# Six-piece attribute load and adjacency store, issued between the gathers of a graph network kernel

## The chip, the core and the metric

One NeuronCore of a Trainium2 chip runs the whole program. The metric is the time of one execution on the device, in microseconds (us). Engines: PE (TensorE: matmuls and transposes), DVE (VectorE), ACT (ScalarE), POOL (GpSimd), SP (SyncE, which only issues transfers here). They run side by side and meet through semaphores. Transfers that SP issues go to a queue served by the core's 16 DMA engines (the hardware queue, q1 in the profile); the indirect gathers that POOL issues go to another queue of the same 16 engines (q0).

## What is computed

A layer of graph attention, and then a layer that sums neighbours and edge attributes, over N = 6250 nodes and E = 200,000 edges sorted by target node, 128 channels:

```python
h = relu(layernorm(x))
xp = (h @ W).reshape(n, 4, 32)
e = leaky_relu(a_s[src] + a_d[dst]); alpha = softmax of e over the edges of each dst
x = x + relu(segment_sum(alpha * xp[src], dst) + bias)           # with a self loop per node
h = relu(layernorm(x))
edge_agg = segment_sum(edge_attr @ We + be, dst)
x_comb = concat([h, edge_agg]);  neigh = segment_sum(x_comb[src], dst)
x = x + relu((x_comb + neigh) @ W1 + b1) @ W2 + b2
```

## The kernel before, in words

After a preparation (node table, logits, masks) the kernel works through the sorted edges in NG = 87 groups of GE = 2304 edges, J = 18 edges for each of the 128 partitions. The targets of a group lie in a window of 128 consecutive nodes. Two sets of buffers alternate, b = n mod 2. The first stage (this is where the change lies) does for group n:

- POOL, `gather` (L768): 18 indirect gathers of 128 table rows of 576 B each into V[b] (L776). The burst for group m may refill a third of V[b] when PE has finished the same third of group m-2 (semaphore vm_b, once each six gathers). So beside group n runs the burst of group n+1.
- DVE, `item`: opens the group with the copy into thru4 (L1554), builds the selection matrix (L1400), the marks for the adjacency, the running maximum of the logits (L1569, then L1578 after PE's transpose L1085, then L1583 after PE's L1087), the new peak of each node (L1614 to L1621, after PE's L1098), looks up the shifts and scales the gathered rows (L1667).
- PE, `item`: adjacency products c = 0 to 5 (L1066), transposes L1085 and L1087, the first half of the attribute sums (L1056, selection times attribute rows), the peak merge (L1098, 18 small matmuls), adjacency 6 to 11, the second half of the attribute sums (its last increments am_b), the lookups (L1110), the weighted sums (L1122, in thirds, each increments vm_b), adjacency 12 to 17.
- ACT: copies the adjacency products from PSUM into adjw[b] (semaphore ab_ev, 18 a group; the last six of group n run at the start of group n+1), and the exponentials.
- SP, `item` (L526): every transfer of the stage, in the order of the program. One wait holds everything behind it.

SP's order for group n before the change: peak and dlogit of the window (L472, L473), the rel rows (L477), store the sums of n-1 (L495, when they are merged), store the new peak of n (L482, when DVE has it: mnew_b), the indices of group n+2 (L440, when the gathers of n have landed), the attributes of group n+2 (L443, 1152 KB, 9216 B for each partition, when am_b of n says that the buffer is free), load the sums (L488) and x (L491), store the residual and the projection of earlier groups (L501, L506), store the adjacency of group n-1 (L510, 1543.5 KB, 12348 B for each partition).

A second stage reads the 87 adjacency blocks back and multiplies them with the second layer's rows. It starts when all stores have landed (adj_out). The blocks named "extra" aren't executed with these inputs.

Of the kernel before, what the change touches and what calls it, by code (L numbers as in the profile page):

```python
# [25 lines left out]
J = 18  # L26
# [29 lines left out]
QUART = J // QN  # L56
FIN = 18
MAGIC = 0x5f3759df
ST = TAB + C
# [12 lines left out]
FARHI = 1 << 20  # L72
assert COLS <= 128 and OFF <= 256 and NB * 128 <= NPAD and GE == J * 128
YCH = ((0, 13), (13, 25), (25, 37), (37, 49))
# [3 lines left out]
def gnn_kernel(nc, x, src, dst, attr, W, att_src, att_dst, bias0, We, be, W1, b1, W2, b2, out):  # L78
    ctx = ExitStack()
    with ctx:  # L80
# [213 lines left out]
        def s(name):  # L294
            if name not in S:
                S[name] = sem(name)
            return S[name]
# [4 lines left out]
            fj_in fj_f jsel_b colr_b dl dl_done tab0_out peak_out tab_out sp_turn idx0 idx1 gat0 gat1  # L302
            attr0 attr1 g_started st_load m_store s_load s_store xw_load sel_b drx_b selc_b thru4_b thruT_b
            thru_c cont_b log_b pre1_b tailT_b tails_b cback_b carry_b pre2_b pkl_b pk_b mg_b mgs_b mnew_b nu_b
# [65 lines left out]
        def _(sp):  # L370
# [65 lines left out]

            def load_edges(n, b, it, start):
                after_dma(sp, s(f"gat{b}"), it * J)
                sp.sem_inc(s("sp_turn"), 1)
                sp.dma_start(idx[b][:, :], src[bass.DynSlice(start, GE)].rearrange("(p j) -> p j", j=J))\  # L440
                    .then_inc(s(f"idx{b}"), 16)
                after(sp, s("am_b"), n, 2)
                sp.dma_start(AT[b], attr[bass.DynSlice(start, GE), :].rearrange("(p j) c -> p j c", j=J))\  # L443
                    .then_inc(s(f"attr{b}"), 16)

            sp.sem_inc(s("y_out"), 16)
            for b in range(2):
                load_edges(b, b, 0, b * GE)

# [57 lines left out]

            def store_adjacency(n, b):
                sp.wait_ge(s("ab_ev"), n * J + J)
                sp.dma_start(adj[bass.DynSlice(n, 1), :, :].rearrange("a p c -> (a p) c"), adjw[b].bitcast(BF16))\  # L510
                    .then_inc(s("adj_out"), 16)
# [14 lines left out]
            def item(n, b, it):  # L526
                base = base_of(n)
                load_peak(n, b, base)
                load_rows(n)
                before_first = isinstance(n, int) and n == 0  # L530
                if not before_first:
                    base_before = base_of(n - 1)
                    store_sums(n - 1, base_before)
                store_peak(n, b, base)
                if not isinstance(n, int) or n + 2 < NG - 1:
                    load_edges(n + 2, b, it + 1, (n + 2) * GE)
                elif n + 2 == NG - 1:
                    load_edges(n + 2, b, it + 1, LAST)
                if before_first:
                    sp.wait_ge(s("tab_out"), 32 * (TAB_CHUNKS + 1))  # L540
                load_sums(n, base)
                if not before_first:
                    store_residual(n - 1, base_before)
                if not (isinstance(n, int) and n < 2):
                    store_projected(n - 2, base_of(n - 2))
                if not before_first:
                    store_adjacency(n - 1, 1 - b)

# [11 lines left out]
            store_residual(NG - 1, base)  # L560
            store_adjacency(NG - 1, 0)
            store_projected(NG - 1, base)
# [14 lines left out]

            sp.wait_ge(s("adj_out"), 16 * NG)
            load_adjacency(0, 0)
# [44 lines left out]
            def extra_item(n, b, it):  # L624
                load_edges(n, b, it, extra(sp, 2, n, LAST))
                base = extra(sp, 1, n, N)
                load_peak(n, b, base)
                store_peak(n, b, base)
                load_sums(n, base, True)
                store_sums(n, base)  # L630
                sp.wait_ge(s("s_store"), n * 16 + 16)
                sp.sem_inc(s("sp_turn"), 1)
# [41 lines left out]
        def _(pool):  # L674
# [93 lines left out]
            def gather(b, it, rows, table, index, gat, ix, n=None):  # L768
                pool.wait_ge(s(f"{ix}{b}"), it * 16 + 16)
                pool.sem_inc(s("g_started"), 1)  # L770
                for j in range(J):
                    if n is not None and j % QUART == 0 and not (isinstance(n, int) and n < 2):

                        pool.wait_ge(s("vm_b"), n * QN + (j // QUART + 1 - 2 * QN))
                        pool.sem_inc(s("g_started"), 1)
                    pool.indirect_dma_start(  # L776
# [15 lines left out]
            with pool.If(uncovered(pool) > 0):  # L792
                extra_pairs(pool, item)
                pool.wait_ge(s("tab1_out"), 64)
                pool.sem_inc(s("g_started"), 1)
                for b in range(2):
# [5 lines left out]
                extra_pairs(pool, first_item2)  # L802
                pool.sem_inc(s("g_started"), 1)


        @block.scalar
        def _(act):
# [59 lines left out]
            def item(n, b, it, is_extra=False):  # L867
# [10 lines left out]
                if not is_extra:  # L878
                    after_dma(act, s("adj_out"), n - 1)
                    keep_adjacency(n, b, 0, 12)  # L880
# [64 lines left out]
        def _(pe):  # L945
# [106 lines left out]
            def item(n, b, it, is_extra=False):  # L1052
# [37 lines left out]
                after(pe, s("selc_b"), n)  # L1090
                pe.wait_ge(s(f"attr{b}"), it * 16 + 16)
                after(pe, s("merged"), n, 2)
# [715 lines left out]
```

## Time and profile before

| | us |
|---|---|
| timed runs, median of 3 | 4222.09 (4209.79 to 4226.62) |
| the profiled execution | 4203.44, of it span 4200.3 |
| the first stage's groups | first opened at 120.8, last at 3391.1 |
| mean granted TensorE clock | 0.745 of full speed |

| engine | busy us | share of the span |
|---|---|---|
| PE | 2634.0 | 63% |
| PE weight loads | 2099.8 | 50% |
| DVE | 1797.7 | 43% |
| POOL | 1652.3 | 39% |
| ACT | 1001.7 | 24% |
| DMA, SP's queue / POOL's queue | | 36.1% / 13.2% of 16 engines |

How to read it: no engine is busy most of the time, so shares say little; what counts is who waits for whom inside a group. A timeline row has start, duration, engine, line, operation, output<-input and how many were merged, and in square brackets the idle time before it and what ended it ("issue": nothing that the profile shows; "remote": a semaphore whose sender it can't name). Times in the text such as +11.1 are counted from the opening copy L1554 of the group in question.

### The profile page before, as it was taken

What the parts mean: (1) busy time and instruction counts of PE and PEld (TensorE: products, weight loads), DVE (VectorE), ACT (ScalarE), POOL (GpSimd) and SP (SyncE); (2) the same over time, 40 slices, a digit from 0 to 9 for tenths busy, and PEclk for the clock granted to TensorE, in tenths of its full rate; (3) what the DMA queues carried; (4) which work ended last, traced back from release to release, by engine and by line L of the source; (5) the groups of instructions that cost most, each with busy time, mean ns of one, the idle gap of its engine ahead of it and who ended that gap; (6) DMA issues with size and microseconds to landing.
All of it is one profiled execution on the core that took longest, in us unless ns stands there. A gap on an engine that the chain in (4) does not pass through costs nothing.

```text
span 4200.3 us, 62157 instructions
## 1 busy us (share of the span) xinstructions
PE 2634.0 (63%) x16749; PEld 2099.8 (50%) x16749; DVE 1797.7 (43%) x6117; ACT 1001.7 (24%) x2335; POOL 1652.3 (39%) x1625
## 2 busy tenths in 40 slices
PE   3455555555555555565555555555555559999999
PEld 2343444444444444444344444444444448888887
DVE  6444454445454444444445444444444541111111
ACT  2223223222222222222222222232222230000000
POOL 4544544454444444544455444544454410000000
PEclk7667676667666676666777776667666779999999
DMA  9444444444443444444444444444444446666665
GB/s 183 113 133 123 141 145 143 126 127 143 145 138 116 141 136 130 133 142 137 124 137 145 144 136 124 140 140 136 123 141 144 135 157 221 215 213 221 215 213 180
DMA packets 309819, 630.10 MB, mean 150 GB/s; under 512 B 115675, under 2 KB 239191, under 8 KB 276133
## 3 DMA queue, kind: packets, MB, share of 16 engines
q1 hardware_dynamic: 259679, 514.22, 36.1%
q0 software_dynamic: 50112, 115.56, 13.2%
q8 instruction: 11, 0.18, 0.0%
q14 instruction: 17, 0.14, 0.0%
HBM read 446.35 MB, written 183.24 MB: 150 GB/s over the span
## 4 chain that ended last, share of the span: by engine, by line
PE 42%; another core or an unknown queue 23%; issue 16%; DVE 9%; ACT 5%; SPq 3%; DMA 1%; DVEq 0%; ACTq 0%
PE pv L1184 11%; PE pv L1122 10%; PE pv L1056 8%; PE pt L1184 5%; ACT xsb L809 5%; PE pt L1066 3%; DVE big L1667 2%; PE pa L1066 1%; DVE lks L1650 1%; DVE tabb L1400 1%; PE pa L1110 1%; PE pm L1098 1%; DVE lin L1654 1%; DVE lin L1659 0%
## 5 line engine op out<-in xcount | busy, mean ns | idle before, releaser
L776 POOL DMA_INDIRECT big<-table,idx x1566 | 1615.6, 1032 | 1698.4 <-PE pv L1122 1220.0
L809 ACT ACTIVATE xsb<-pt 128x343 bf16<-128x343 f32 x1044 | 531.5, 543 | 1987.3 <-PE pt L1066 1029.0
L1066 PE MATMUL pt<-tabb 128*128 128x343 bf16 x1044 | 395.4, 381 | 819.9 <-ACT xsb L809 461.6
L1066 PEld LDWEIGHTS pt<-tabb 128*128 128x128 bf16 x1044 | 105.4, 101 | 1053.4 <-ACT xsb L809 577.5
L1056 PE MATMUL pv<-big 128*128 128x128 f32 x3132 | 629.4, 386 | 0.0
L1056 PEld LDWEIGHTS pv<-big 128*128 128x128 f32 x3132 | 613.0, 299 | 1.5
L1122 PE MATMUL pv<-big 128*128 128x133 f32 x3132 | 498.6, 326 | 162.3 <-DVE big L1667 162.3
L1122 PEld LDWEIGHTS pv<-big 128*128 128x128 f32 x3132 | 470.9, 234 | 182.9 <-DVE big L1667 175.5
L1184 PE MATMUL pv<-big,xsb 128*126 128x384 bf16 x2842 | 493.8, 327 | 19.0 <-DVE big L1695 19.0
L1184 PEld LDWEIGHTS pv<-big,xsb 128*126 128x126 bf16 x2842 | 382.8, 136 | 88.2 <-issue 19.0
L1400 DVE TENSOR_TENSOR tabb<-iotah,keyp 128x2064 bf16<-128x2064 bf16 x261 | 320.3, 1227 | 1.4 <-issue 1.1
L1578 DVE TENSOR_TENSOR_SCAN tails<-thruT,pm 4x128 f32<-4x128 f32 x87 | 35.6, 409 | 618.5 <-issue 293.8
L1614 DVE TENSOR_SCALAR pen<-pm 128x1 f32<-128x1 f32 x87 | 13.7, 158 | 665.0 <-remote 549.6
L809 ACT ACTIVATE xsb<-pa 128x343 bf16<-128x343 f32 x522 | 280.2, 537 | 24.6 <-PE pt L1066 12.5
L1184 PE MATMUL pt<-big,tabb 128*126 128x384 bf16 x1421 | 248.4, 326 | 0.0
L1667 DVE TENSOR_TENSOR big<-big,pm 128x768 f32<-128x768 f32 x261 | 233.4, 950 | 26.1 <-ACT pm L809 26.1
L1066 PE MATMUL pa<-tabb 128*128 128x343 bf16 x522 | 199.1, 381 | 40.1 <-issue 28.6
L1710 DVE TENSOR_TENSOR fy<-pa,fxw 128x128 f32<-128x128 f32 x87 | 25.4, 292 | 454.2 <-PE pa L1167 454.2
L1098 PE MATMUL pm<-peaks,selb 128*128 128x13 bf16 x1566 | 72.8, 171 | 226.2 <-issue 191.7
L1184 PEld LDWEIGHTS pt<-big,tabb 128*126 128x126 bf16 x1421 | 190.8, 136 | 33.8
L809 ACT ACTIVATE fhT<-pt,b1s 128x128 f32<-128x128 f32 x87 | 31.9, 367 | 707.1 <-PE pt L1161 707.1
L809 ACT ACTIVATE big<-selb 128x2304 f32<-128x2304 bf16 x87 | 183.2, 2106 | 0.6 <-issue 0.6
(271 smaller groups left out, 2584.0 us busy)
## 6 DMA issues: line engine op xcount, KB each, us to landing
adj<-xsb SPq DMA_DIRECT2D x87, 1543.5 KB
big<-in_edge_attr_dram SPq DMA_DIRECT2D x87, 1152.0 KB, 5.2
xsb<-adj SPq DMA_DIRECT2D x58, 1543.5 KB, 6.7
selb<-rel SPq DMA_DIRECT2D x87, 576.0 KB
tabb<-adj SPq DMA_DIRECT2D x29, 1543.5 KB, 6.7
big<-table,idx POOLq DMA_INDIRECT x1566
state<-sums SPq DMA_DIRECT2D x87, 130.5 KB
sums<-state SPq DMA_DIRECT2D x87, 130.5 KB
```

The lines of the kernel that those rows point to most:

```text
L776: pool.indirect_dma_start(out=V[b][:, j, 0:rows], out_offset=None, in_=table, in_offset=bass.IndirectOffsetOnAxis(ap=index[b][:, j:j + 1], ...
L809: return nc.scalar.activation(out_, in_, func, **kw).then_inc(s(name), 1)
L1056: ins = nc.tensor.matmul(sumA[b], SEL[b][:, j, :], AT[b][:, j, :], start=(j == 0), stop=(j == J - 1))
L1066: nc.tensor.matmul(pab[c % 3], ohl[:, c, :], ohk[:, c, 0:KW], start=True, stop=True)\
L1098: ins = nc.tensor.matmul(mg, selH[:, j, :], peaks[:, j, :], start=(j == 0), stop=(j == J - 1))
L1110: ins = nc.tensor.matmul(lk[:, j, :], selT[:, j * 128:(j + 1) * 128], parts[b], start=True, stop=True)
L1122: ins = nc.tensor.matmul(sumV[b], SEL[b][:, j, :], V[b][:, j, 0:TAB], start=(j == 0), stop=(j == J - 1))
L1184: ins = nc.tensor.matmul(pay[k][0:COLS, 0:NK * C], adjT[k][:, h, :], yb[:, h, :], start=(h == 0), stop=(h == NB - 1))
L1400: return v.tensor_tensor(to.rearrange("p j (w e) -> p j w e", e=2), v_in, at, ALU.is_equal)
L1650: v.tensor_reduce(lks[:, :, :].rearrange("p j (g h) -> p (j g) h", h=H), lk.rearrange("p j (g k h) -> p (j g) h k", k=NK, h=H), AX.X, ALU. ...
L1654: v.tensor_tensor(lin[:, :, :], V[b][:, :, C:C + H], lks[:, :, 0:H], ALU.add).then_inc(s("lks_b"), 1)
L1667: v.tensor_tensor(v4, v4, wps[:, js, :].rearrange("p j (h a) -> p j h a", a=1) .to_broadcast([128, QUART, H, F]), ALU.mult).then_inc(s("vw ...
```

## The change

The attribute load and the adjacency store become six transfers each: attributes by three of the 18 j (1536 B for each partition, 192 KB), adjacency by a sixth of the columns (2058 B for each partition, 257.25 KB). They are issued in pairs. Pair 0 follows the sums store; pair i waits until the burst beside the group has begun its i-th step of three gathers (new semaphore g_step, which POOL increments before every third gather, in place of the increments of g_started that nothing waited for). Pairs 0 to 2 stand before the wait for the new peak (L482), pairs 3 to 5 behind the index load. The attributes that are loaded beside group n are now those of group n+1 (before: of n+2), and the adjacency stored is that of n-1, as before. Waits on both semaphores are multiplied by six.

```diff
-            def load_edges(n, b, it, start):
+            def load_index(b, it, start):
                 after_dma(sp, s(f"gat{b}"), it * J)
                 sp.sem_inc(s("sp_turn"), 1)
                 sp.dma_start(idx[b][:, :], ...).then_inc(s(f"idx{b}"), 16)
-                after(sp, s("am_b"), n, 2)
-                sp.dma_start(AT[b], attr[bass.DynSlice(start, GE), :].rearrange("(p j) c -> p j c", j=J))\
+            def load_attr(b, start, i):
+                js = slice(i * PJ, (i + 1) * PJ)
+                sp.dma_start(AT[b][:, js, :], attr[...].rearrange("(p j) c -> p j c", j=J)[:, js, :])\
                     .then_inc(s(f"attr{b}"), 16)
...
-            def store_adjacency(n, b):
-                sp.wait_ge(s("ab_ev"), n * J + J)
+            def store_adjacency(n, b, i):
+                if i == 0:
+                    sp.wait_ge(s("ab_ev"), n * J + J)
+                cs = slice(i * (NB * COLS // APIECES), (i + 1) * (NB * COLS // APIECES))
...
+                last = isinstance(n, int) and n == NG - 1
+                following = 0 if last else LAST if isinstance(n, int) and n == NG - 2 else (n + 1) * GE
+                def spread(lo, hi):
+                    for i in range(lo, hi):
+                        if not last:
+                            if i > 0:
+                                sp.wait_ge(s("g_step"), n * PIECES + (PIECES + i))
+                            elif not before_first:
+                                after(sp, s("am_b"), n, 1)
+                            load_attr(1 - b, following, i)
+                        if not before_first and i * APIECES % PIECES == 0:
+                            store_adjacency(n - 1, 1 - b, i * APIECES // PIECES)
+                spread(0, PIECES // 2)
                 store_peak(n, b, base)
-                if not isinstance(n, int) or n + 2 < NG - 1:
-                    load_edges(n + 2, b, it + 1, (n + 2) * GE)
-                elif n + 2 == NG - 1:
-                    load_edges(n + 2, b, it + 1, LAST)
+                if not isinstance(n, int) or n + 2 < NG:
+                    load_index(b, it + 1, LAST if isinstance(n, int) and n + 2 == NG - 1 else (n + 2) * GE)
+                spread(PIECES // 2, PIECES)
...
-                if not before_first:
-                    store_adjacency(n - 1, 1 - b)
...
             def gather(b, it, rows, table, index, gat, ix, n=None):
                 pool.wait_ge(s(f"{ix}{b}"), it * 16 + 16)
-                pool.sem_inc(s("g_started"), 1)
+                pool.sem_inc(s("sp_turn"), 1)
                 for j in range(J):
                     if n is not None and j % QUART == 0 and not (isinstance(n, int) and n < 2):
                         pool.wait_ge(s("vm_b"), n * QN + (j // QUART + 1 - 2 * QN))
-                        pool.sem_inc(s("g_started"), 1)
+                    if j % PJ == 0:
+                        pool.sem_inc(s("g_step"), 1)
...
-                    after_dma(act, s("adj_out"), n - 1)
+                    after_dma(act, s("adj_out"), n * APIECES - APIECES)
...
-                pe.wait_ge(s(f"attr{b}"), it * 16 + 16)
+                pe.wait_ge(s(f"attr{b}"), (it * 16 + 16) * PIECES)
```

## Rows read from the trace of the kernel before

**Rows 1.** The line that opens each group: count, duration ns, first and last start.

```profile
L1554 DVE COPY thru<-thru x87: 162/164/173, 120.8 to 3391.1; 128x4 f32 x84, 128x4 f32<-128x4 f32 x3
```

**Rows 2.** Timeline of an ordinary group, opened at 2026.52, all engines.

```profile
2026.52 0.16 DVE L1554 COPY thru<-thru 128x4 f32 x1
2027.35 1.52 POOL L776 DMA_INDIRECT big<-table,idx  x1 [13.62 <-PE pv L1122]
...
2031.81 0.60 ACT L809 ACTIVATE xsb<-pt 128x343 bf16<-128x343 f32 x1
...
2037.64 0.22 DVE L1583 SCALAR_TENSOR_TENSOR logit<-pm,cin,logit 128x4 f32<-128x4 f32 x1 [0.29 <-issue]
...
2040.93 0.60 PE L1098 MATMUL pm<-peaks,selb 128*128 128x13 bf16 x18
...
2050.34 0.94 POOL L776 DMA_INDIRECT big<-table,idx  x1 [0.30 <-issue]
2053.78 0.16 DVE L1614 TENSOR_SCALAR pen<-pm 128x1 f32<-128x1 f32 x1 [10.79 <-remote]
```

**Rows 3.** The waits of the whole span: total us, times, longest.

```profile
POOL big L776 <- PE pv L1122: 1220.0, 85, 22.5
...
SPq L482 <- DVE newold L1621: 1760.2, 79, 27.6
```

**Rows 4.** Timeline of DVE in the last group.

```profile
3391.08 0.16 DVE L1554 COPY thru<-thru 128x4 f32<-128x4 f32 x1
...
3409.89 0.16 DVE L1614 TENSOR_SCALAR pen<-pm 128x1 f32<-128x1 f32 x1
```

**Rows 5.** Timeline of SP in the same ordinary group.

```profile
2026.22 0.33 SPq L510 DMA_DIRECT2D adj<-xsb  x1
...
2031.47 0.36 SPq L495 DMA_DIRECT2D sums<-state  x1
2054.35 0.35 SPq L482 DMA_DIRECT2D peak<-newold  x1
2055.07 0.35 SPq L440 DMA_DIRECT2D idx<-in_src_dram  x1
2058.74 0.35 SPq L443 DMA_DIRECT2D big<-in_edge_attr_dram  x1
2060.36 0.33 SPq L488 DMA_DIRECT2D state<-sums  x1
```

**Rows 6.** DMA issues: count, KB each, us from issue to landing.

```profile
big<-in_edge_attr_dram SPq DMA_DIRECT2D x87, 1152.0 KB, 5.2
```

**Rows 7.** Windows of the ordinary group: length, busy times, PEclk, DMA share, GB/s.

```profile
2030.50:2035.80 5.30, 2.83 (x10) 0.98 (x11) 0.59 (x2) 5.30 (x11) 3.79 (x5) 0.79 0.85 222
...
2037.60:2053.70 16.10, 4.97 (x39) 4.18 (x39) 5.34 (x20) 0.00 (x0) 10.64 (x11) 0.61 0.22 52
```

**Rows 8.** The group opened at 151.27: two windows, and DVE's L1583.

```profile
151.27:152.77 1.50, 1.50 (x8) 1.50 (x8) 1.50 (x5) 0.00 (x0) 0.00 (x0) 0.50 1.06 395
152.77:157.30 4.53, 4.07 (x31) 3.10 (x30) 2.78 (x8) 1.55 (x5) 3.13 (x3) 1.00 0.13 30
...
163.37 0.23 DVE L1583 SCALAR_TENSOR_TENSOR logit<-pm,cin,logit 128x4 f32<-128x4 f32 x1 [0.24 <-PE pm L1087]
```

**Rows 9.** The group opened at 1220.51: one gather, and the next opening.

```profile
1220.51 0.16 DVE L1554 COPY thru<-thru 128x4 f32 x1
...
1235.23 2.33 POOL L776 DMA_INDIRECT big<-table,idx  x1 [0.30 <-issue]
...
1253.98 0.16 DVE L1554 COPY thru<-thru 128x4 f32 x1
```

**Rows 10.** The group opened at 877.49: DVE's L1578, and the next opening.

```profile
877.49 0.16 DVE L1554 COPY thru<-thru 128x4 f32 x1
...
902.17 0.41 DVE L1578 TENSOR_TENSOR_SCAN tails<-thruT,pm 4x128 f32<-4x128 f32 x1 [18.50 <-remote]
...
920.26 0.16 DVE L1554 COPY thru<-thru 128x4 f32 x1
```

More of the change, by code:

```diff
@@ L57 @@
 FIN = 18
+PIECES = 6
+PJ = J // PIECES
+APIECES = 6
 MAGIC = 0x5f3759df
@@ L72 @@
 FARHI = 1 << 20
-assert COLS <= 128 and OFF <= 256 and NB * 128 <= NPAD and GE == J * 128
+assert J % PIECES == 0 and NB * COLS % APIECES == 0 and COLS <= 128 and OFF <= 256 and NB * 128 <= NPAD and GE == J * 128
 YCH = ((0, 13), (13, 25), (25, 37), (37, 49))
@@ L302, in gnn_kernel @@
             fj_in fj_f jsel_b colr_b dl dl_done tab0_out peak_out tab_out sp_turn idx0 idx1 gat0 gat1
-            attr0 attr1 g_started st_load m_store s_load s_store xw_load sel_b drx_b selc_b thru4_b thruT_b
+            attr0 attr1 g_step st_load m_store s_load s_store xw_load sel_b drx_b selc_b thru4_b thruT_b
             thru_c cont_b log_b pre1_b tailT_b tails_b cback_b carry_b pre2_b pkl_b pk_b mg_b mgs_b mnew_b nu_b
@@ L441, in load_edges @@
                     .then_inc(s(f"idx{b}"), 16)
-                after(sp, s("am_b"), n, 2)
-                sp.dma_start(AT[b], attr[bass.DynSlice(start, GE), :].rearrange("(p j) c -> p j c", j=J))\
+            def load_attr(b, start, i):
+                js = slice(i * PJ, (i + 1) * PJ)
+                sp.dma_start(AT[b][:, js, :], attr[bass.DynSlice(start, GE), :].rearrange("(p j) c -> p j c", j=J)[:, js, :])\
                     .then_inc(s(f"attr{b}"), 16)
@@ L447, in _ @@
             for b in range(2):
-                load_edges(b, b, 0, b * GE)
+                load_index(b, 0, b * GE)
+            for i in range(PIECES):
+                load_attr(0, 0, i)
             for lo, hi in ((0, SPLIT), (SPLIT, NP)):
@@ L506, in store_projected @@
                 sp.dma_start(sums1[bass.DynSlice(base, WIN), :], fy[:, :]).then_inc(s("y_out"), 16)
-            def store_adjacency(n, b):
-                sp.wait_ge(s("ab_ev"), n * J + J)
-                sp.dma_start(adj[bass.DynSlice(n, 1), :, :].rearrange("a p c -> (a p) c"), adjw[b].bitcast(BF16))\
+            def store_adjacency(n, b, i):
+                if i == 0:
+                    sp.wait_ge(s("ab_ev"), n * J + J)
+                cs = slice(i * (NB * COLS // APIECES), (i + 1) * (NB * COLS // APIECES))
+                sp.dma_start(adj[bass.DynSlice(n, 1), :, cs].rearrange("a p c -> (a p) c"), adjw[b].bitcast(BF16)[:, cs])\
                     .then_inc(s("adj_out"), 16)
@@ L560, in _ @@
             store_residual(NG - 1, base)
-            store_adjacency(NG - 1, 0)
+            for i in range(APIECES):
+                store_adjacency(NG - 1, 0, i)
             store_projected(NG - 1, base)
@@ L576, in load_residual @@
                 sp.dma_start(fxw[:, :], resid[bass.DynSlice(base, WIN), :]).then_inc(s("xr_load"), 16)
-            sp.wait_ge(s("adj_out"), 16 * NG)
+            sp.wait_ge(s("adj_out"), 16 * APIECES * NG)
             load_adjacency(0, 0)
@@ L624, in extra_item @@
             def extra_item(n, b, it):
-                load_edges(n, b, it, extra(sp, 2, n, LAST))
+                start = extra(sp, 2, n, LAST)
+                load_index(b, it, start)
+                after(sp, s("am_b"), n, 2)
+                for i in range(PIECES):
+                    load_attr(b, start, i)
                 base = extra(sp, 1, n, N)
@@ L794, in _ @@
                 pool.wait_ge(s("tab1_out"), 64)
-                pool.sem_inc(s("g_started"), 1)
+                pool.sem_inc(s("sp_turn"), 1)
                 for b in range(2):
@@ L802, in _ @@
                 extra_pairs(pool, first_item2)
-                pool.sem_inc(s("g_started"), 1)
+                pool.sem_inc(s("sp_turn"), 1)
         @block.scalar
```

## The prediction

> **What bounds the kernel now.** I read four views in this order: the DVE instruction that opens each group (how long a group takes), the waits (who holds whom), the timeline of one ordinary group across all engines, and the same stretch cut into windows (what the DMA queues do meanwhile). The opening copy L1554 runs 87 times from 120.8 to 3391.1 us [rows 1], so a group of the first stage takes (3391.1 - 120.8) / 86 = 38.0 us, and 86 of them are 3270 of the 4200 us span. The change touches only this stage.
>
> In the group that opens at 2026.52 the gather burst (for the next group) starts at +0.8 and its last gather is issued at +23.8 [rows 2]. PE behaves until L1087, for whose result DVE's L1583, at +11.1, has been idle only 0.3 us. Then it stops delivering: the eighteen L1098 matmuls are dispatched by +15.0, yet DVE L1614, which needs only them, starts at +27.3, 2.5 us after the last gather instruction has ended. Everything queued behind comes at once. Over all groups the waits say the same from the other ends [rows 3]: POOL stands 1220 us in 85 waits for PE's L1122, about 14.4 us a group between bursts, and SP stands 1760 us at L482, for the new peak that hangs on L1614. So this is a ring: burst, release of PE at its end, the tail of the group up to L1122, next burst.
>
> That the burst holds PE, and not the work itself, is seen in the last group, beside which no burst runs [rows 4]: L1614 comes at 3409.89 - 3391.08 = +18.8, against +27.3. The stall is worth 27.3 - 18.8 = 8.5 us a group, on the path. No row gives a cause for it: the releasers are put down as remote or as issue.
>
> **The change part by part, on SP's order.** Today SP issues the adjacency store of 1543 KB just before a group opens (2026.22), then the peak, dlogit and rel loads and the sums store (2031.47), then waits for the new peak (L482, 2054.35), loads the index (2055.07) and, after the second half of L1056 the attributes (2058.74) [rows 5]. After it, pieces 0 to 2 of both transfers stand behind the sums store, pieces 3 to 5 behind the peak store and the index load.
>
> *Pieces 0 to 2.* They need am_b of the group before (done), all its adjacency evacuations (the last is the ACT copy at 2031.81, over by +5.9 [rows 2]) and at most the second step of the burst, which begins with the fourth gather, near +5. So 3 x 192 + 3 x 257 = 1348 KB goes out from about +6. Each DMA instruction takes 0.35 us, and peak store to index load are 0.72 us apart [rows 5]; by that row six take 6 x 0.72 = 4.3 us, so SP is free near +10. What is queued behind is the wait for the peak, which comes at +27.3: 17 us of cover, cost nothing. If the stall went away the peak would come near +18.8, and the cover would still be 8 us.
>
> *Pieces 3 to 5.* **Here the change doesn't do what its name says.** The program order puts L482's wait ahead of them, and that wait ends at +27.8 (2054.35), 4 us after the last gather was issued. The steps they wait for are long past, and they go out back to back from +29 to about +33. The peak store and the index load keep their time. Behind them stands load_sums, which today waits for other things until 2060.36, that is +33.8; I take 0, with up to 0.5 us on the bad side (the six would have to take over 0.8 us each). The attribute load lands 5.2 us after issue as a whole [rows 6]; even if the late half took all of that it would be in by +38, and its reader comes after L1087 of the next group, 10 us later. The stored buffer's next writer, the ACT evacuation, is in the next group, which opens at +38, against an issue that ends at +33: about 5 us of cover. If that is gone, each us costs a us.
>
> *What moves away.* The attribute load and the whole store leave the stretch from -4.9 to +4. It is the stretch in which all queues are busiest (395 GB/s in the first 1.5 us of the group at 151.27, [rows 8]); the rel load and the peak loads no longer queue behind the store. None of these transfers is waited for today, so I take 0 here, between -0.5 and +0.5 us a group (a gather's start follows L1122 of the group before, not a queue).
>
> *PE's wait, ACT's wait.* Same instructions with other constants: 0. *POOL:* six semaphore increments in place of four a burst, on an engine that stands 0.30 us between gathers [rows 2], which holds all such bookkeeping. Two more at a sixth of that each are 0.1 us a burst, an estimate; PE holds POOL back once a burst anyway. So 0 taken, 85 x 0.1 = 9 us at the bad end. *Start and end:* the second group's attributes are no longer loaded ahead, and are needed late; 0. The last store is cut into six in front of the second stage: 5 more instructions at 0.6 us (between the 0.35 and the 0.72 above), +3 us.
>
> **Sum.** 86 groups at 0, +3 us at the end. Against the profiled execution's own 4203.4 us that is 4206 us. The median of the timed runs stands 4222.1 - 4203.4 = 18.7 us above it, so 4225 us. Bounds of the small terms, -0.5 to +1 us a group, give 4180 to 4310 for this case.
>
> **What decides: does other DMA traffic change PE's stall?** In the ordinary group the SP queue is busy until about +9 (222 GB/s in the window to 2035.80) and PE delivers; from 2037.60 to 2053.70 only gathers run, 52 GB/s, and PE delivers nothing [rows 7]. That fits *quiet SP queue, slow PE*. Against it stands the group that opens at 151.27: all queues together move 30 GB/s from +1.5 to +6, and DVE's L1583 still follows L1087 at +12.1 after 0.24 us of idleness [rows 8]. A gather that takes 2.33 us instead of 0.94 (group at 1220.51) goes with a group of 33.5 us [rows 9]: what differs there is the gathers' cadence, and the change leaves that alone.
>
> The Trainium skill, page *SBUF — State Buffer*, section *SBUF: two separate sides*, says that engine ports and DMA ports are disjoint, so that PE never waits on anyone. By that rule moving DMA traffic could do nothing to PE, and the result would be the 4225 above. The trace agrees in part only: PE does stall while gathers run, so I don't put the other cases at nothing.
>
> **Rivals.**
> *Faster: SP traffic keeps PE awake.* The quiet window [rows 7] speaks for it, the group at 151.27 [rows 8] against. If pieces 0 to 2, which end near +10 to +12 rather than +9, carry PE past L1098 (+15 is needed), the peak comes early, pieces 3 to 5 then fall into the burst, and the ring opens. Full effect: 85 x 8.5 = 722 us, 4225 - 722 = 3503. Part of it, as in the 33.5 us group: 38.0 - 33.5 = 4.5 us, x 85 = 385, 3840.
> *Slower: the chain L1085 to L1087 misses the good stretch.* It ends at +11.1 with the stall beginning at about +12. If 1348 KB in short rows beside the first gathers (today the two streams overlap less) slows PE's deliveries, L1085 is answered only when the burst ends, as in the group at 877.49: DVE's L1578 waits 18.5 us there and starts at +24.7, and the group takes 920.26 - 877.49 = 42.8 us, 4.8 more [rows 10]. It decides once L1085 is later by about 1 us. All groups: 85 x 4.8 = 408, 4633; a third of them, 4360.
> *The change doesn't do what it says*, because of L482: this is my forecast, not a rival.
>
> **How the numbers follow.** Forecast case 0.62, faster rival 0.20 (half full, half in part), slower rival 0.18. A measurement of this kernel tells about 0.5% (21 us) from no change, only 0.25 us a group, so the forecast case itself splits: within 0.34, slower 0.16, faster 0.12. Sums: faster 0.32, same 0.34, slower 0.34. The range goes down to the partial effect, 3800 (leaves out 0.10), and up to 4450 (leaves out the slower rival over more than half the groups, 0.06); the forecast case's own range is 4180 to 4310.
>
> **What would show it.** Right: L443's pieces in two clumps, three near +6 to +10 and three after L482 near +29; L1614 still some 3.5 us after the last gather's start; POOL's wait for L1122 near 1220 us. Wrong on the fast side: L1614 near +19, L482's total well under 1760 us and pieces 3 to 5 inside the burst. Wrong on the slow side: L1085 to L1578 taking 5 us or more in many groups, and groups of 42 us no longer rare. Wrong in a small term: L488 waiting behind the pieces, or ACT idle before its first evacuation with a store as releaser.

## The result, and the profile after

The changed kernel takes 4253.35 us (median of 9 runs, 4237.28 to 4260.46) against 4222.06 us (median of 9, 4204.80 to 4242.50) for the kernel before. The ratio is 1.0074, with a 95% interval of 1.0050 to 1.0098: slower by 31 us, or 0.7%. The profiled execution took 4253.35 us, of it span 4251.8.

The opening copy, the waits of the whole span and SP's own waits, where [rows 1] and [rows 3] have those of before (lines from here on are the changed kernel's, 27 higher on PE, ACT, POOL and DVE, 3 to 9 higher on SP: L1554 is now L1581, L1614 is L1641, L1122 is L1149, L776 is L803, L482 is L489):

```profile
L1581 DVE COPY thru<-thru x87: 159/164/169, 115.8 to 3436.8; 128x4 f32 x84, 128x4 f32<-128x4 f32 x3
```

```profile
POOL big L803 <- PE pv L1149: 1275.9, 85, 21.2
```

```profile
SPq L489 <- DVE newold L1648: 644.9, 85, 19.3
```

A group takes (3436.8 - 115.8) / 86 = 38.6 us, where it took 38.0. The 86 groups are 3321.0 us against 3270.3, and this difference of 50.7 is that of the two profiled executions (4253.4 - 4203.4 = 49.9; the execution that was traced before lies 19 us below its median, so the medians differ by less, 31 us). So all of it is in the first stage. POOL waits 55.9 us longer in the same 85 waits for PE: the ring of burst, release and tail has become longer, and not by a longer burst, since POOL's gathers were busy 1606.8 us, against 1615.6 before. SP's wait for the new peak, on the other hand, has shrunk from 1760.2 to 644.9 us. SP is now doing something for 1115 us, 13 us a group, in which it used to stand.

What it is doing stands in the timeline of a group that opens at 2007.80, here without most rows of DVE, ACT and PE:

```profile
2007.80 0.16 DVE L1581 COPY thru<-thru 128x4 f32 x1
2010.03 1.73 POOL L803 DMA_INDIRECT big<-table,idx  x1 [14.87 <-PE pv L1149]
...
2014.56 0.94 POOL L803 DMA_INDIRECT big<-table,idx  x1 [0.30 <-issue]
...
2029.68 0.48 PEld L1125 LDWEIGHTS pm<-peaks,selb 128*128 128x128 bf16 x15 [2.63 <-issue]
...
2032.11 0.10 PEld L1125 LDWEIGHTS pm<-peaks,selb 128*128 128x128 bf16 x1 [1.95 <-issue]
2032.34 1.11 POOL L803 DMA_INDIRECT big<-table,idx  x1 [0.31 <-issue]
2033.54 0.17 PE L1125 MATMUL pm<-peaks,selb 128*128 128x13 bf16 x1 [1.99 <-issue]
2034.97 0.10 PEld L1125 LDWEIGHTS pm<-peaks,selb 128*128 128x128 bf16 x1 [2.76 <-issue]
...
2036.77 0.16 DVE L1641 TENSOR_SCALAR pen<-pm 128x1 f32<-128x1 f32 x1 [4.14 <-PE pm L1125]
```

and of SP in the same group:

```profile
2014.49 0.35 SPq L502 DMA_DIRECT2D sums<-state  x1
2015.03 0.52 SPq L448 DMA_DIRECT2D big<-in_edge_attr_dram  x1
2017.76 0.01 SPq L519 DMA_DIRECT2D adj<-xsb  x1
2020.63 0.01 SPq L448 DMA_DIRECT2D big<-in_edge_attr_dram  x1
2024.20 0.73 SPq L519 DMA_DIRECT2D adj<-xsb  x1
2029.24 0.71 SPq L448 DMA_DIRECT2D big<-in_edge_attr_dram  x1
2033.50 0.73 SPq L519 DMA_DIRECT2D adj<-xsb  x1
2037.34 0.35 SPq L489 DMA_DIRECT2D peak<-newold  x1
2037.97 0.35 SPq L443 DMA_DIRECT2D idx<-in_src_dram  x1
2038.57 0.35 SPq L448 DMA_DIRECT2D big<-in_edge_attr_dram  x1
...
2041.35 0.36 SPq L519 DMA_DIRECT2D adj<-xsb  x1
```

The six transfers of pieces 0 to 2 start over 18.5 us (2015.03 to 2033.50), the six of pieces 3 to 5 over 2.8 us. The gather steps are not what holds the first ones. The last step that they wait for began with the fourth gather, at 2014.56, and the store of piece 2 goes out 19 us later. It is each SP instruction that is slow. The same line has, besides its transfer, a register operation and a move; the source view of L519 for 2014 to 2036 gives their durations (ns, minimum, median, maximum):

```profile
L519 SPq FUSED_REGOPS  x3: 37/691/691, 2016.6 to 2030.7; - x3
L519 SPq MOVE adj<-xsb x3: 710/722/727, 2017.0 to 2032.1; - x3
L519 SPq DMA_DIRECT2D adj<-xsb x3: 5/727/728, 2017.8 to 2033.5; - x3
```

and for 2036 to 2045, when the burst is over:

```profile
L519 SPq FUSED_REGOPS  x3: 37/37/37, 2039.0 to 2041.2; - x3
L519 SPq MOVE adj<-xsb x3: 29/29/29, 2039.1 to 2041.3; - x3
L519 SPq DMA_DIRECT2D adj<-xsb x3: 355/356/356, 2039.1 to 2041.3; - x3
```

The same move takes 0.72 us beside the burst and 0.03 after it, and the profile shows nothing that it waits for. This isn't one group's luck. Of the moves and register operations that SP executes between the first and the last gather of a burst, 525 of 1610 take over 300 ns in the whole trace; of the others, 15 of 3762 do. Before the fifth us of a burst they are rare (6 of 595), between the eighth and the tenth they are the larger part (82 of 132).

PE's L1125 has the same gait: idle 1.95 to 2.76 us before single small matmuls, put down to "issue". So what I had called PE's stall isn't PE's alone: while a long burst runs, instructions of SP and of PE are slow. It isn't seen on every engine. DVE's chain from L1583 to L1607 (of before), which lies in the same burst, has a median of 2.44 us in the kernel before, in the changed kernel and in a run of it without any slow SP instruction (after_third, below).

Two windows of the same group answer [rows 7] (length, busy times, granted clock, DMA share, GB/s):

```profile
2015.00:2020.80 5.80, 3.15 (x10) 0.91 (x10) 0.00 (x0) 5.80 (x12) 4.28 (x6) 0.84 0.67 181
2020.80:2033.50 12.70, 5.43 (x35) 5.00 (x36) 5.96 (x24) 0.15 (x1) 9.90 (x10) 0.50 0.42 122
```

In the stretch in which only the gathers' 52 GB/s ran before, 122 GB/s run now, and PE is held all the same.

### The profile page after: what moved, and what is told of

It is laid out like the page before. It is cut to its first block, busy times and chain, and to the rows that moved or that the text cites. A ratio compares the mean times of both kernels' runs of the same rounds, so it can differ in the third digit from the quotient of the medians.

```text
span 4251.8 us, 65303 instructions
## 1 busy us (share of the span) xinstructions
PE 2679.3 (63%) x16749; PEld 2134.7 (50%) x16749; DVE 1801.3 (42%) x6117; ACT 993.1 (23%) x2335; POOL 1643.5 (39%) x1625
## 4 chain that ended last, share of the span: by engine, by line
PE 46%; issue 20%; another core or an unknown queue 19%; DVE 7%; ACT 6%; DMA 0%; ACTq 0%; SPq 0%; DVEq 0%
PE pv L1211 11%; PE pv L1083 10%; PE pv L1149 9%; PE pt L1211 5%; ACT xsb L836 5%; PE pt L1093 4%; PE pa L1093 2%; DVE big L1694 2%; DVE lks L1677 1%; PE pa L1137 1%; PE pm L1125 1%; DVE tabb L1427 1%; DVE lin L1681 1%; DVE lin L1686 1%
## 5 line engine op out<-in xcount | busy, mean ns | idle before, releaser
L803 POOL DMA_INDIRECT big<-table,idx x1566 | 1606.8, 1026 | 1751.6 <-PE pv L1149 1275.9
L1093 PE MATMUL pt<-tabb 128*128 128x343 bf16 x1044 | 405.0, 390 | 748.1 <-ACT xsb L836 355.2
L1083 PE MATMUL pv<-big 128*128 128x128 f32 x3132 | 642.8, 392 | 0.0
L1083 PEld LDWEIGHTS pv<-big 128*128 128x128 f32 x3132 | 626.8, 305 | 1.5
L1149 PE MATMUL pv<-big 128*128 128x133 f32 x3132 | 517.8, 335 | 162.2 <-DVE big L1694 162.2
L1149 PEld LDWEIGHTS pv<-big 128*128 128x128 f32 x3132 | 489.9, 242 | 182.9 <-DVE big L1694 175.4
L1641 DVE TENSOR_SCALAR pen<-pm 128x1 f32<-128x1 f32 x87 | 13.7, 158 | 666.0 <-remote 497.4
L1605 DVE TENSOR_TENSOR_SCAN tails<-thruT,pm 4x128 f32<-4x128 f32 x87 | 35.6, 409 | 594.3 <-issue 367.2
L1125 PE MATMUL pm<-peaks,selb 128*128 128x13 bf16 x1566 | 74.1, 171 | 310.4 <-issue 288.6
L1125 PEld LDWEIGHTS pm<-peaks,selb 128*128 128x128 bf16 x1566 | 59.7, 98 | 298.9 <-issue 285.4
```

What stands on the lines that cost most here:

```text
L803: pool.indirect_dma_start(out=V[b][:, j, 0:rows], out_offset=None, in_=table, in_offset=bass.IndirectOffsetOnAxis(ap=index[b][:, j:j + 1], ...
L1083: ins = nc.tensor.matmul(sumA[b], SEL[b][:, j, :], AT[b][:, j, :], start=(j == 0), stop=(j == J - 1))
L1093: nc.tensor.matmul(pab[c % 3], ohl[:, c, :], ohk[:, c, 0:KW], start=True, stop=True)\
L1125: ins = nc.tensor.matmul(mg, selH[:, j, :], peaks[:, j, :], start=(j == 0), stop=(j == J - 1))
L1149: ins = nc.tensor.matmul(sumV[b], SEL[b][:, j, :], V[b][:, j, 0:TAB], start=(j == 0), stop=(j == J - 1))
```

## The experiments

Each kernel was run beside the kernel before on the same chip. The level of the kernel before itself turned out to differ between these comparisons: some 4200 us in some, 3395 us in others (35 and 25 runs, all within 3385 to 3403), and once both on the same chip, some 13 minutes apart. Only the ratio inside one comparison is used; it is taken over the runs and can differ by a little over 0.1% from the quotient of the two medians. Where the kernel before takes 3395 us, I write "without the stall"; the trace of after_third below shows why.

| kernel | before beside it, us | this, us | ratio, 95% interval |
|---|---|---|---|
| changed kernel (the result) | 4222.06 | 4253.35 | 1.0074, 1.0050 to 1.0098 |
| after_again (the same) | 4197.96 | 4157.87 | 0.9911, 0.9879 to 0.9942 |
| after_third (the same) | 3395.02 | 3395.87 | 1.0002, 0.9993 to 1.0012 |
| late_all | 3394.60 | 3392.47 | 0.9999, 0.9990 to 1.0008 |
| late_again | 3395.02 | 3395.41 | 1.0002, 0.9992 to 1.0011 |
| early_all | 3394.60 | 3394.31 | 1.0003, 0.9993 to 1.0013 |
| two_whole | 3394.60 | 3393.71 | 1.0001, 0.9991 to 1.0011 |
| probe_only | 3394.60 | 3397.16 | 1.0009, 0.9999 to 1.0019 |
| thin_rows | 3395.02 | 3394.02 | a single run |
| half_gathers | 4197.96 | 3420.62 | a single run |
| hold_thirds | 3395.02 | 3392.40 | 0.9995, 0.9985 to 1.0004 |
| hold_again (the same) | 4181.99 | 4089.35 | 0.9774, 0.9727 to 0.9822 |
| hold_half | 4197.51 | 3835.06 | 0.9125, 0.9081 to 0.9168 |

**Where in the group, and by what? Four kernels beside one another.** late_all puts all twelve pieces behind the index load:

```diff
-                spread(0, PIECES // 2)
                 store_peak(n, b, base)
...
-                spread(PIECES // 2, PIECES)
+                spread(0, PIECES)
```

> All twelve pieces behind the index load, none in the burst. Theory A (bytes): the pieces' traffic beside the gathers delays PE's release after the last gather (4.16 us after its start in the changed kernel against 3.66). Theory B (turns): SP's own instructions during the burst, each 0.7 us instead of 0.03 to 0.35, compete with PE's for the same supply. Both expect the time of the kernel before, 4222 us, ratio 1.000 +- 0.002. Theory C (late half): what costs are pieces 3 to 5 behind L482; then this one is slower than the changed kernel, ratio 1.010 or more.

early_all puts them all ahead of the peak store:

```diff
-                spread(0, PIECES // 2)
+                spread(0, PIECES)
                 store_peak(n, b, base)
...
-                spread(PIECES // 2, PIECES)
```

> All twelve pieces ahead of the wait for the new peak, so that the step waits really pace them. A: three more pairs of traffic beside the last gathers, so the cost doubles, ratio 1.015. B: twice as many SP instructions in the burst; at 1.4 us an instruction SP can't finish them in the burst and reaches the peak store some 3 us after it, near +30; ratio 1.010 to 1.020. C: 1.000. If pacing were worth what its name suggests, below 0.99.

two_whole issues one whole load and one whole store at the place of the first pair, without step waits (the waits on the two semaphores are set back to one transfer; those lines are left out here):

```diff
-                js = slice(i * PJ, (i + 1) * PJ)
+                js = slice(0, J)
...
-                cs = slice(i * (NB * COLS // APIECES), (i + 1) * (NB * COLS // APIECES))
+                cs = slice(0, NB * COLS)
...
-                spread(0, PIECES // 2)
+                spread(0, 1)
...
-                spread(PIECES // 2, PIECES)
```

> The attribute load and the adjacency store as one transfer each at the place of piece 0, with nothing later: the same bytes, beside the burst, by 2 DMA instructions in place of 12. B: six SP instructions in the burst and over before PE's stall begins: ratio 1.000 to 1.002. A, if any bytes beside the gathers count: 1.007 or more; if only bytes beside the last gathers: 1.000, since 2696 KB at some 220 GB/s are out by +18.

probe_only leaves the transfers of the kernel before where they are and adds instructions alone (PROBES is 7; POOL counts its steps as in the changed kernel):

```diff
+                if not (isinstance(n, int) and n == NG - 1):
+                    for i in range(1, 6):
+                        sp.wait_ge(s("g_step"), n * 6 + (6 + i))
+                        for _ in range(PROBES):
+                            sp.sem_inc(s("sp_turn"), 1)
                 store_peak(n, b, base)
```

> The kernel before, with POOL's step increments and five step waits on SP, each followed by 7 semaphore increments that nobody reads; no transfer is moved. In the burst these 40 instructions show what an SP instruction costs there without any DMA: 0.7 to 1.4 us each if the supply is slow (theories A and B both see that in the changed kernel), 0.03 us otherwise. A: ratio 1.000. B: more SP instructions in the burst than the 20 or so of the changed kernel, so at least its cost, 1.007 to 1.015.

Measured: ratios of 0.9999, 1.0003, 1.0001 and 1.0009, with the kernel before at 3394.60 us and not at 4222. For telling theory A from B the four were in vain, since what they were to vary wasn't there. What they do show is that without the stall nothing in this change costs or gains 0.2%: not the place of the pieces, not their number, not the bytes beside the gathers. Theory C, a cost of pieces 3 to 5 on their own, falls for that case too; with the stall none of the four was measured, so there A, B and C aren't told apart.

**The changed kernel itself, twice more.** after_again and after_third are the changed kernel word for word.

> The changed kernel itself, word for word, beside the kernel before on the same chip. In the four runs so far neither kernel showed the stall beside the gathers (3395 us, where the recorded runs show 4222). Theory D: the change costs only where the stall is there, since only there is an SP instruction in the burst slow; without the stall the ratio is 1.000 +- 0.002, with it 1.007. Theory E: the cost is the change's own and independent of the stall: 1.007 of 4222 is 31 us, so 3426 us, ratio 1.009, without it.

> The changed kernel once more, as the yardstick beside the two next. Its ratio was 1.007 in the recorded runs and 0.991 on another chip, both with the stall beside the gathers. Theory F: the change's effect has no sign of its own; it is how the stall's steps of 0.7 us fall, which differs from chip to chip: anything from 0.985 to 1.015 here if the stall is there, 1.000 if it isn't. Theory G: the change costs 0.7% wherever the stall is, and 0.991 came from something else: 1.005 to 1.010 again.

Beside a kernel before of 4198 us it was faster, 0.9911; beside one of 3395 us the same, 1.0002. D holds for the second, and E, which expected 1.009 there, falls. D's other half, 1.007 with the stall, doesn't hold, nor does G: the sign turned, with intervals far apart. F is what is left, though it says only where the effect lives and not how it comes about; that it goes by the chip is not shown, since the record doesn't name the chip of the first comparison. The changed kernel alone took 4253 us in one comparison with the stall and 4158 in another, 2.3% apart, and the stall differs between the two traces as well: in after_again 352 of the 1697 moves and register operations of SP inside bursts take over 300 ns, against 525 of 1610. So 0.7% between two kernels is less than what the stall does to one of them from one comparison to the next. after_third shows the group without the stall:

```profile
L1581 DVE COPY thru<-thru x87: 161/163/170, 118.1 to 2585.6; 128x4 f32 x84, 128x4 f32<-128x4 f32 x3
```

```profile
L519 SPq MOVE adj<-xsb x492: 29/29/29, 177.7 to 2521.0; - x164
```

```profile
2011.33 0.16 DVE L1581 COPY thru<-thru 128x4 f32 x1
...
2024.04 0.23 DVE L1610 SCALAR_TENSOR_TENSOR logit<-pm,cin,logit 128x4 f32<-128x4 f32 x1 [0.35 <-PE pm L1114]
2029.11 0.15 DVE L1641 TENSOR_SCALAR pen<-pm 128x1 f32<-128x1 f32 x1
```

```profile
2017.42 0.33 SPq L448 DMA_DIRECT2D big<-in_edge_attr_dram  x1
...
2021.23 0.36 SPq L519 DMA_DIRECT2D adj<-xsb  x1
```

```profile
POOL big L803 <- PE pv L1149: 409.9, 85, 7.1
```

Not one of the 492 moves takes more than 29 ns. L1641 comes at 2029.11 - 2011.33 = +17.8, the pieces 0 to 2 are issued in 3.8 us, a group takes (2585.6 - 118.1) / 86 = 28.7 us, and POOL waits 410 us instead of 1276. The gathers are the same 18, at the same 1.25 us. No move or register operation of SP in the groups takes over 163 ns. This is the same program without the slow instructions, and their absence is worth 4253 - 3396 = 858 us, or 4158 - 3396 = 762 us against after_again.

late_again was late_all once more, hoping for the stall:

> All twelve pieces behind the index load, so nothing of the change lies in the burst. Where the stall is there: if it is pieces 0 to 2 beside the gathers that shift the time, this one has the time of the kernel before, ratio 0.997 to 1.003, while the changed kernel beside it differs. If the traffic moved away from the group's opening matters instead, this one moves as the changed kernel does. Without the stall 1.000, as before.

It met none (1.0002). So whether the pieces beside the gathers shift the time within the stall was not tried with success, and stays open.

**What the stall hangs on: fewer gathers.** half_gathers drops nine of the 18 gathers of a group (its waits for the gathers' landing are lowered to match; those lines are left out here):

```diff
+                    if n is not None and not (isinstance(n, int) and n < 2) and j >= 9:
+                        continue
                     pool.indirect_dma_start(
```

> The kernel before, with only the first 9 of the 18 gathers of each group from the third on (the rows of the other 9 j stay those of earlier groups, so values are not the reference's). If the burst holds PE for as long as it runs, the last 8.5 us of stall go: 4222 - 85 x 8.5 = 3500 us. If the stall isn't there (3395 us for the kernel before), the burst of 24 us lies beside a group of 28.7 us, and halving it gives at most what POOL's wait leaves: 3390 if PE's chain is the bound, some 3300 if gathers and PE still touch somewhere.

3420.62 us in a single run, where the kernel before took 4197.96 (median of 13) and 3500 was expected. Nearly all of the stall went, and not only the last 8.5 us of it. A single run could have met the level without the stall by chance, but its trace still has marks of the stall: SP's longest moves and register operations in the groups take 316, 304, 302 and 301 ns, where none of the eight traces without the stall has one over 163, and L1583 comes after +15 in 42 of 84 groups (as late as +16.8), where in after_third it never comes after +14.0. So the stall was most likely about, and nine gathers left little of it. The run drops gathers, bytes and the length of the burst together and doesn't tell them apart. thin_rows kept the number and cut the bytes, in all groups from the third on:

```diff
+                    thin = n is not None and not isinstance(n, int)
                     pool.indirect_dma_start(
-                        out=V[b][:, j, 0:rows], out_offset=None, in_=table,
+                        out=V[b][:, j, C:rows] if thin else V[b][:, j, 0:rows], out_offset=None,
+                        in_=table.rearrange("n (a c) -> (n a) c", c=rows - C) if thin else table,
```

> The kernel before, where the gathers of each group from the third on take 64 B of each row in place of 576 (values aren't the reference's): the same number of gathers and rows, a ninth of the bytes. If the stall hangs on the bytes that the gathers move, it goes: about 3420. If it hangs on the number of gathers, rows or their cadence, it stays: 4150 to 4250. Without the stall: 3395.

It met no stall (3394.02 beside 3395.02) and so says nothing on bytes against number.

**Cutting the burst.** hold_thirds makes POOL wait twice, on things that happen anyway:

```diff
+                    if n is not None and j == 6:
+                        after(pool, s("carry_b"), n, 1)
+                        pool.sem_inc(s("g_started"), 1)
+                    if n is not None and j == 12:
+                        after(pool, s("mg_b"), n, 1)
+                        pool.sem_inc(s("g_started"), 1)
                     pool.indirect_dma_start(
```

> The kernel before, with POOL's burst cut in two places: gathers 6 to 11 wait until DVE L1583 of the group beside has run, 12 to 17 until PE's L1098 is answered. With half of the gathers the stall was gone altogether (3421 us against 4198), so it needs a long burst. If a pause of some 3 us breaks it: L1614 near +18 in place of +27, a group of 29 to 32 us, 3450 to 3700 us. If only gathers in all count: 4200. Without the stall the pause can only cost: 3395 to 3500.

> The kernel with the burst cut in two places, once more: without the stall it cost nothing (ratio 0.9995, 95% interval 0.9985 to 1.0004). Where the kernel before takes some 4200 us: if a pause breaks what builds up during a long burst, L1614 comes near +18 to +22 in place of +27, SP's instructions beside the gathers take 0.03 us again until late in the burst, and the whole takes 3450 to 3800 us (ratio 0.82 to 0.90). If the number of gathers in a group sets the stall, whatever the pauses, 4150 to 4300 us (0.98 to 1.02).

Without the stall it cost nothing, 0.9995. With it, 0.9774 (0.9727 to 0.9822), which lies just under the range expected if pauses are of no use (0.98 to 1.02) and far from the other (0.82 to 0.90). The group that opens at 2017.94 says why (L1589 is L1583 of before, L1620 is L1614, L1656 the reader of the lookups):

```profile
2017.94 0.16 DVE L1560 COPY thru<-thru 128x4 f32 x1
...
2032.04 0.22 DVE L1589 SCALAR_TENSOR_TENSOR logit<-pm,cin,logit 128x4 f32<-128x4 f32 x1 [0.35 <-PE pm L1093]
2038.89 0.16 DVE L1620 TENSOR_SCALAR pen<-pm 128x1 f32<-128x1 f32 x1 [1.72 <-remote]
2050.71 0.61 DVE L1656 TENSOR_REDUCE lks<-pa 128x144 f32<-128x432 f32 x1 [7.04 <-PE pa L1116]
2055.26 0.16 DVE L1560 COPY thru<-thru 128x4 f32 x1
```

```profile
2033.06 0.95 POOL L782 DMA_INDIRECT big<-table,idx  x1 [4.89 <-DVE logit L1589]
...
2047.41 0.95 POOL L782 DMA_INDIRECT big<-table,idx  x1 [0.31 <-issue]
```

The first part of the gain is there: L1620 at +21.0, not +27. But the second of the two waits is over when POOL comes to it, so the other twelve gathers run without a pause from 2033.06 to 2048.4: the burst is cut into 6 and 12 and not into thirds. Now it is the lookups that come only 2.4 us after the burst has ended, after 7.04 us of idleness. The stall has moved on by one step, and a group still takes 37.3 us (35.5 to 37.8 in all 84 ordinary groups).

hold_half cuts once, in the middle, so that neither part is longer than the nine that had run with hardly any stall:

```diff
+                    if n is not None and j == 9:
+                        after(pool, s("mg_b"), n, 1)
+                        pool.sem_inc(s("g_started"), 1)
                     pool.indirect_dma_start(
```

> The kernel before with the burst cut once: gathers 9 to 17 wait until PE's L1098 is answered (some 6 us of pause). Where the stall is there: a burst of 9 gathers alone left no stall (3421 us), and with the cuts at 6 and 12 the last 12 gathers ran without a pause and it came back in their second half, over the lookups L1110 (a group of 37 us). If what builds up is undone by a pause of 5 us, no stretch here is long enough: a group of 29 to 31 us, 3420 to 3600 us, ratio 0.82 to 0.86. If the pause doesn't undo it, the second nine hold PE back as before: 4000 to 4150 us. Without the stall, where the kernel before takes 3395 us, the last gather is issued near +29, 1 to 3 us later than its use allows: 3400 to 3550 us, ratio 1.00 to 1.05.

3835.06 us beside 4197.51, ratio 0.9125: the fastest of the kernels that compute all and were run with the stall, 362 us ahead of the kernel before. It lies between the two cases expected (3420 to 3600 and 4000 to 4150). Two of its groups (L1617 is L1614 of before, L1653 the reader of the lookups), and between them the gather behind the pause and the last gather, both beside the first group:

```profile
2035.14 0.16 DVE L1557 COPY thru<-thru 128x4 f32 x1
...
2052.89 0.15 DVE L1617 TENSOR_SCALAR pen<-pm 128x1 f32<-128x1 f32 x1
2064.07 0.61 DVE L1653 TENSOR_REDUCE lks<-pa 128x144 f32<-128x432 f32 x1 [7.42 <-remote]
2068.61 0.16 DVE L1557 COPY thru<-thru 128x4 f32 x1
```

```profile
2052.52 1.27 POOL L779 DMA_INDIRECT big<-table,idx  x1 [3.41 <-PE pm L1101]
...
2062.89 0.95 POOL L779 DMA_INDIRECT big<-table,idx  x1 [0.31 <-issue]
```

```profile
2103.93 0.16 DVE L1557 COPY thru<-thru 128x4 f32 x1
...
2123.08 0.15 DVE L1617 TENSOR_SCALAR pen<-pm 128x1 f32<-128x1 f32 x1
...
2127.86 0.61 DVE L1653 TENSOR_REDUCE lks<-pa 128x144 f32<-128x432 f32 x1 [0.99 <-PE pa L1113]
...
2132.40 0.29 DVE L1557 COPY thru<-thru 128x4 f32 x1
```

L1617 comes at +17.8 and +19.2, as without the stall. In the second group the lookups follow 4.8 us later and the group takes 28.5 us. In the first they come 11.2 us later, 0.2 us after its last gather has ended, and it takes 33.5 us. Without the stall the lookups come 6 us after that line (after_third, on average), so in the first group the hold began within some 6 us of the second nine gathers' start. Over the trace 25 of 84 groups take under 31 us, as without the stall, and the median is 35.2. A pause (3.4 us here, 3.3 to 5.2 us in three quarters of the groups) therefore undoes only in part whatever nine gathers leave behind. How much hold_half costs without the stall was not measured.

## Why the prediction was right or wrong

The forecast was 4225 us, the measured time is 4253 (ratio 1.0074), inside the forecast case's own range of 4180 to 4310. The time was near, by way of a sum whose terms were partly wrong.

*What bounds the kernel.* The ring of burst, release and tail was read rightly, and the stall's size too: 8.5 us a group from the last group, which has no burst, where the comparison of the two levels gives (4222 - 3395) / 86 = 9.6. What it is was read wrongly. I took it for PE not delivering. SP's row in the changed kernel shows a move of 0.72 us where it takes 0.03. The kernel before could hardly show it, since SP stood at L482 through most of the burst: of 3650 moves and register operations on SP only 10 take over 300 ns. Nor does PE behave until L1087 in every group, as I had read from the one in [rows 2]: L1583 comes after +15 in 34 of 84 groups of the kernel before.

*Pieces 0 to 2: the step that failed.* "By that row six take 6 x 0.72 = 4.3 us, so SP is free near +10", with 17 us of cover behind it. They took 18.5 us in the group above, to +25.7, and 3.5 to 19.4 us over the groups, with a median of 14.3, because the price came from a row after the burst. The conclusion "cost nothing" survived: of the cover of 17 us a median of 8.7 us was left, but 1.7 us in the tightest group (SP's wait at L489 fell by 1115 us, 13 us a group), and SP still stood there in 85 waits of 87 groups, so the peak store was hardly ever late. At 18.5 / 5 = 3.7 us from one transfer to the next, three more would have used up the cover of most groups, an estimate. Without the stall the step holds to the letter: in after_third the six take 3.8 us and the cover left is 8.0 us, the 8 us forecast for that case.

*Pieces 3 to 5.* As forecast: held by the wait for the peak, issued from 2038.57 to 2041.35, 5 to 8 us after the last gather has ended. The sums load follows at 2044.40, waiting for others: SP's wait for PE's L1072 stands in 86 groups, 155.2 us in all, more than the 101.7 us before, so these pieces held nothing up. That the change doesn't do what its name says held for half of it; for the other half its pace was set by slow instructions and not by g_step.

*What moves away, waits of PE and ACT, POOL's increments, the end.* Without the stall all of these together are 1.0002, with an interval up to 1.0012, so 0 was right for them within 4 us. One count was wrong, at no cost: POOL has seven increments a burst in place of four, not six (sp_turn once and g_step six times), and its gathers still stand 0.30 to 0.32 us apart where they follow an increment.

*The term that was mis-sized* is the one that had no line in the sum: that the stall stays exactly as long as it was. The time lost, 50.7 us in 86 groups or 0.59 us a group, lies in the ring's wait for PE (+55.9 us in POOL's 85 waits). In the group above the last gather starts at 2032.34 and L1641 at 2036.77, 4.4 us later, against 3.4 us in [rows 2]; over 84 groups the mean is 4.15 us against 3.65, while the last gather starts at +24.3 in both. That is 0.50 of the 0.59 us. I had allowed -0.5 to +1 us for the small terms, and this fits in only because that allowance was wide: that the forecast came within 28 us of the result is luck as far as this term goes. Since the same kernel was faster by 0.9% in another comparison, with the stall there as well, I can't call 0.6 us its cost. There the same distance is 3.32 us. What moves is the end of the stall, and what sets its sign was not found.

*The faster rival* (traffic of SP's queue keeps PE awake) is refuted, at the sizes that it had, by the changed kernel itself: 122 GB/s in the stalled window and PE idle 2 to 2.8 us before single matmuls. The group at 151.27 [rows 8], which I had held against it, was the better witness than the quiet window [rows 7].

*The slower rival* (L1085 to L1087 slip into the stall) happened in the group shown above, but no oftener than before: L1583 of before comes after +15 in 34 of 84 groups there and in 33 here, and DVE's idle time before the scan L1578 fell from 618.5 to 594.3 us over the span. It is not where the time went.

*The rule on ports, and instruction fetch.* The Trainium skill, page *SBUF — State Buffer*, section *SBUF: two separate sides*, has engine and DMA ports disjoint, and by it moved traffic couldn't do anything to PE. The trace agrees in this: more than twice the DMA traffic in the window (122 against 52 GB/s), and PE held as before. Another page of the Trainium skill, *Runtime: NRT & Kernel Launch*, section *Instruction fetch mechanics*, says that instructions are fetched ahead in blocks by a DMA queue and that a taken branch out of the window stalls. The changed kernel's profile has 11 and 22 packets on the two instruction queues in its whole span, that of late_all without the stall 11 and 21. In the changed kernel none of them falls between 270 and 3400 us, the stretch of nearly all groups. So no fetch once a group or once a gather is seen there, and the slow instructions aren't explained by it.

## What to carry to other kernels

A price read from one stretch of the trace doesn't hold in another: ask of each instruction that is moved what the same engine's cheapest instructions (a move, a register operation) take in the stretch it is moved to. Where engines seem frozen beside a long run of indirect gathers, cut the run with waits on events that come anyway: one cut of 18 into 9 and 9 was worth 8.8% here, one into 6 and 12 2.3%, and the latter was free where there was no stall. An effect of 1% that lives inside such a stall should be measured where it is there and where it isn't before a reason is written beside it.

## What was not expected of the hardware

- A run of 18 indirect gathers of 128 rows can slow instructions on SP and PE: an SP move took 710 to 727 ns instead of 29, in the group above from 7 us after the first gather (2010.03 to 2017.0) to the end of the burst. DVE's chain in the same bursts kept its 2.44 us.
- The same program, on the same chip, ran with this (4198 us) and without it (3395 us; in the changed kernel every move of L519 29 ns). What decides which was not found, nor whether it hangs on bytes or on the number of rows. All the times here come with the profiler's span and clock, so whether the stall exists when nothing is recorded isn't known either.
- Nine gathers in a run of 11 us left hardly any stall (3421 us, a single run). Nine, a pause of 3 to 5 us and nine more left it in most groups (3835 us, 59 of 84 groups over 31 us); six, a pause and twelve in all (4089 us).
